# The end of a fused cross-attention and expert layer: stores by tile, softmax sums ahead of values, rows turned by DMA, an indirect gather before the real ones

## What is computed

```python
x = x + tanh(g_xattn) * xattn(layernorm(x), ctx, ctx)      # 16 heads of 32; scores, softmax, values
#     out -> mean over 8 experts of (out @ We[e].T + be[e]) -> @ Wo.T + bo
x = x + tanh(g_ffn) * ffn(layernorm(x))
# ffn: probs = softmax(hs @ w_gate); best = argmax(probs)       (8 experts)
#      the first 100 tokens (in order over all batches) that choose an expert get
#      gate * (hs @ w_expert + b_expert); all others get 0
```

## Time and profile before

| | |
|---|---|
| median of 3 runs | 458.92 us (458.69 to 459.90) |
| the profiled execution | 459.45 us |
| its span | 457.7 us |
| TensorE busy | 431.4 us (94%) |
| DVE busy | 343.7 us (75%) |
| ScalarE busy | 223.4 us (49%) |
| POOL busy | 158.6 us (35%) |
| mean granted TensorE clock | 0.981 |

### The profile page before, as it was taken

The page is one execution under the profiler, slowest core; times in us unless marked ns, Lnnn a source line. Parts: engine busy times, 40 slices in busy tenths (PEclk is TensorE's granted clock), DMA queues, the critical chain, the costliest instruction groups (busy, mean ns, idle before and its releaser), DMA issues.

```text
span 457.7 us, 8305 instructions
## 1 busy us (share of the span) xinstructions
PE 431.4 (94%) x2935; PEld 200.7 (44%) x2935; DVE 343.7 (75%) x670; ACT 223.4 (49%) x278; POOL 158.6 (35%) x147
## 2 busy tenths in 40 slices
PE   5899998899999999999999999999999999499997
PEld 4457564342344344434534443443453444144453
DVE  5448335985597899889879888987983997478873
ACT  4343321556663845666375384656727466451110
POOL 1005899106043319307123430820521161430430
PEclk9997999999999999999999999999999999879999
DMA  8997791048018705923840772593283052230223
GB/s 214 319 391 275 273 399 43 16 108 210 1 30 165 216 19 117 217 93 80 171 176 0 162 179 89 115 189 123 45 168 121 1 117 94 54 90 1 62 65 110
DMA packets 56250, 60.85 MB, mean 133 GB/s; under 512 B 32675, under 2 KB 35887, under 8 KB 56211
## 3 DMA queue, kind: packets, MB, share of 16 engines
q1 hardware_dynamic: 51195, 54.10, 43.5%
q0 software_dynamic: 1536, 3.28, 2.6%
q10 hardware_dynamic: 3480, 2.96, 1.9%
HBM read 29.38 MB, written 12.98 MB: 93 GB/s over the span
## 4 chain that ended last, share of the span: by engine, by line
PE 69%; DVE 12%; issue 10%; ACT 5%; DMA 2%; SPq 0%; DVEq 0%; ACTq 0%; POOLq 0%
PE ps L728 50%; PE ps L405 9%; DVE neg_max L1358 4%; ACT probs L1038 4%; DVE attn L1318 3%; PE ps L367 3%; PE ps L501 3%; DVE q_lo L1352 2%; DMA raw<-in_L_xattn_Wk_dram 1%; DVE rden_both L1313 1%; DMA rows<-out_dram,row_ix 1%; PE ps L989 1%; PE ps L475 1%; PE ps L524 1%; PE ps L931 1%
## 5 line engine op out<-in xcount | busy, mean ns | idle before, releaser
L1038 ACT ACTIVATE probs<-ps 120x2048 f32<-120x2048 f32 x32 | 60.1, 1879 | 41.1 <-PE ps L728 41.1
L1660 POOL TENSOR_TENSOR attn_lo<-attn,attn_hi 128x512 f16<-128x512 f32 x28 | 31.5, 1155 | 114.5 <-ACT attn_hi L1038 114.5
L1358 DVE TENSOR_REDUCE neg_max<-ps 128x16 f32<-128x1920 f32 x32 | 68.6, 2143 | 1.9 <-PE ps L728 1.9
L728 PE MATMUL ps<-xnT_hi,wqT_hi 128*128 128x512 f16 x128 | 48.6, 380 | 1.0 <-issue 0.9
L728 PE MATMUL ps<-mixT_hi,attn_hi 128*128 128x512 f16 x128 | 48.6, 380 | 0.9 <-ACT xnT_hi L1038 0.9
L728 PE MATMUL ps<-mixT_lo,attn_hi 128*128 128x512 f16 x128 | 48.5, 379 | 0.0
L728 PE MATMUL ps<-xnT_lo,wqT_hi 128*128 128x512 f16 x128 | 48.5, 379 | 0.0
L1668 POOL TENSOR_TENSOR xb<-xb,mix_bias 128x512 f32<-128x512 f32 x32 | 39.5, 1265 | 22.4 <-DVE cb_col L1301 22.4
L1605 POOL TENSOR_SCALAR veps<-mv 128x4 f32<-128x4 f32 (+1 forms) x17 | 4.3, 256 | 123.4 <-DVE mv L1247 84.7
L1038 ACT ACTIVATE q_hi<-ps,bias_cols 128x512 f16<-128x512 f32 x32 | 21.9, 684 | 40.1 <-PE ps L728 40.1
L1352 DVE SCALAR_TENSOR_TENSOR q_lo<-ps,bias_cols,q_hi 128x512 f16<-128x512 f32 x32 | 23.9, 746 | 20.7 <-ACT q_hi L1038 20.7
(11 more groups left out here) (242 smaller groups left out, 828.0 us busy)
## 6 DMA issues: line engine op xcount, KB each, us to landing
xb<-in_x_dram SPq DMA_DIRECT2D x8, 1024.0 KB, 5.9
out_dram<-xb SPq DMA_DIRECT2D x7, 1024.0 KB, 6.1
q_stack<-q_hi SPq DMA_DIRECT2D x48, 128.0 KB, 2.4
raw<-in_L_xattn_We_dram SPq DMA_DIRECT2D x5, 1024.0 KB, 12.8
q_stack<-q_lo SPq DMA_DIRECT2D x32, 128.0 KB, 2.4
xb<-in_L_xattn_We_dram SPq DMA_DIRECT2D x3, 1024.0 KB, 11.1
k_stack<-k_scratch SPq DMA_DIRECT2D x8, 360.0 KB, 4.4
ctx_raw<-in_ctx_dram SPq DMA_DIRECT2D x8, 240.0 KB, 7.5
```

Of the source, the lines that this page charges most:

```text
L728: return e.matmul(out_, a, b, start=start, stop=stop, **kw)
L1038: return e.activation(out_, in_, func, **kw)
L1358: e.tensor_reduce(neg_max[:, :, :, g], quad[:, :, 0:NT * SK].rearrange("p j (t s) -> p t j s", t=NT), AX.X, ALU.max, negate=True).then_inc ...
L1660: e.tensor_tensor(attn_lo[:, g, :], attn[:, g, :], attn_hi[:, g, :], ALU.subtract).then_inc(s_alo, 1)
```

## The change

- Stores: batch 6 is stored by tile. Tiles 0 and 1 go ahead of the load of batch 7's shift row, tiles 2 and 3 follow in the next turn of SP's loop.
- TensorE, last batch: `weight_sums` of group 3 stands ahead of `value_sums` of group 2.
- ScalarE: `rden_high` stands ahead of `row_norm` 0.
- Rows 4 to 7 and the four tiles of batch 7 are no longer turned by TensorE. They are split as they lie in SBUF (`row_parts`, `x2_parts`: views of `xn_hi`, `xn_lo` and of `q_stack`), and SP turns them with eight DMA transposes, each for two rows or tiles of one half (`turn_pairs`).
- POOL: `row_ix` is set to 0, and after `add_bias` of batch 7 one indirect gather of row 0 of x is issued (into `rows[:, 0, :]`, written anew by the first real gather); `row_index` and the real gathers wait for it.
- DVE: `enter` is split in `enter_rows` and `enter_places`, the former ahead of `read_places`; `expert_low` is done in two halves, the second after `enter_places` of batch 6; the order of the last batch's steps is another.

```diff
+            def store_tiles(b, tiles):
+                for t in tiles:
+                    e.wait_ge(s_x1, 4 * b + t + 1)
+                    load(out_rows[b][:, t, :], xb[:, b % NX, t, :], s_st)
+
+            def turn_pairs(dst, src, ready, s_):
+                for pair in range(2):
+                    for part in range(2):
+                        e.wait_ge(ready[part][0], ready[part][1] + 2 * pair + 2)
+                        e.dma_start(dst[part][:, 8 * pair:8 * (pair + 1), :],
+                                    src[part].rearrange("p x c -> p (x c)")[:, 8 * P * pair:8 * P * (pair + 1)],
+                                    transpose=True).then_inc(s_[pair][part], 16)
...
-                if 1 <= r < B:
+                if r == B - 1:
+                    store_tiles(B - 2, (2, 3))
+                elif r >= 1:
...
+                    if r == B - 2:
+                        store_tiles(r, (0, 1))
                     e.wait_ge(s_sh, r + 2)
                     load(q_stack[3 * DK:STACK, :, :, :].rearrange("o j g s -> o (j g) s"),
                          shift[:, :], s_rsh)
...
+            e.wait_ge(s_sc, 4 * B)
+            turn_pairs(row_turned, row_parts, ((s_thi, 4), (s_tlo, 4)), s_rowt)
+            turn_pairs(x2_turned, x2_parts, ((s_x2h, 0), (s_x2l, 0)), s_x2t)
...
-                (scores, 0, 3), (weight_sums, 0, 2), (table_rows, -1, 0), (value_sums, 0, 2), (values, 0, 3),
+                (scores, 0, 3), (weight_sums, 0, 2), (table_rows, -1, 0), (weight_sums, 0, 3), (value_sums, 0, 2),
+                (value_sums, 0, 3),
...
-                (row_product, 0, 2), (row_turn, 0, 4), (x2_turn, 0, 0), (row_product, 0, 3), (row_turn, 0, 5),
-                (x2_turn, 0, 1), (row_product, 0, 4), (x2_turn, 0, 2), (row_turn, 0, 6), (row_product, 0, 5),
-                (x2_turn, 0, 3), (row_turn, 0, 7), (row_product, 0, 6), (places, 0, 0), (row_product, 0, 7),
+                (row_product, 0, 2), (row_product, 0, 3), (row_product, 0, 4), (row_product, 0, 5), (row_product, 0, 6),
+                (places, 0, 0), (row_product, 0, 7),
...
             def row_high(_, x_):
+                if x_ >= 4:
+                    e.wait_ge(s_xth, 16 * (B - 1))
+                    e.wait_ge(s_txn, x_ + 1)
+                    act(row_parts[0][0:CAP, x_ - 4, :], row_n[:, x_ % 4, :]).then_inc(s_thi, 1)
+                    return
...
-                (row_norm, 0, 0), (rden_high, 0, 0), (row_high, 0, 0), (row_norm, 0, 1), (attn_high, 0, 0),
+                (rden_high, 0, 0), (row_norm, 0, 0), (row_high, 0, 0), (row_norm, 0, 1), (attn_high, 0, 0),
...
-                (row_high, 0, 2), (row_norm, 0, 3), (row_high, 0, 3), (row_norm, 0, 4), (row_norm, 0, 5),
-                (row_norm, 0, 6), (row_norm, 0, 7), (gate_exp, 0, 0),
-                (row_high, 0, 4), (x2_high, 0, 0), (row_high, 0, 5), (x2_high, 0, 1), (x2_high, 0, 2),
-                (row_high, 0, 6), (x2_high, 0, 3), (row_high, 0, 7),
+                (row_high, 0, 2), (row_norm, 0, 3), (row_high, 0, 3), (row_norm, 0, 4), (row_high, 0, 4),
+                (row_norm, 0, 5), (row_high, 0, 5), (row_norm, 0, 6), (row_high, 0, 6), (row_norm, 0, 7), (row_high, 0, 7),
+                (x2_high, 0, 0), (x2_high, 0, 1), (x2_high, 0, 2), (x2_high, 0, 3), (gate_exp, 0, 0),
...
-                (last_attn_low, 0, 0), (last_attn_low, 0, 1), (divide, 0, 2), (divide, 0, 3), (row_bias, 0, 0),
-                (row_out, 0, 0), (last_attn_low, 0, 2), (last_attn_low, 0, 3), (row_lo, 0, 2), (row_bias, 0, 1),
-                (row_out, 0, 1), (row_lo, 0, 3), (row_bias, 0, 2),
+                (last_attn_low, 0, 0), (last_attn_low, 0, 1), (divide, 0, 2), (divide, 0, 3), (last_attn_low, 0, 2),
+                (last_attn_low, 0, 3), (row_lo, 0, 2), (row_bias, 0, 0), (row_out, 0, 0), (row_lo, 0, 3),
+                (row_bias, 0, 1), (row_out, 0, 1), (row_lo, 0, 4), (row_bias, 0, 2),
+                (x1_tile, 0, 0), (stats2, 0, 0), (moment2, 0, 0), (row_lo, 0, 5), (row_bias, 0, 3),
+                (x1_tile, 0, 1), (route_sum, 0, 0), (stats2, 0, 1), (moment2, 0, 1), (row_lo, 0, 6),
...
             run([B - 2], [(rstd2, -1, 0)] + attn_lows + [(add_bias, 1, 0)])
+            e.wait_ge(s_clr, 2)
+            e.indirect_dma_start(
+                out=rows[:, 0, :], out_offset=None, in_=x_flat[:, :],
+                in_offset=bass.IndirectOffsetOnAxis(ap=row_ix[:, 0:1], axis=0),
+                bounds_check=B * S - 1, oob_is_err=False).then_inc(s_warm, 16)
             run([B - 1], [(rstd2, -1, 0)])
```

More of the change, by code:

```diff
@@ L277, in build @@
         s_x2n = sem("s_x2n")
-        s_x2t = sem("s_x2t")
+        s_x2t = [[sem(f"s_x2t{part}{pair}") for part in ("h", "l")] for pair in range(2)]
+        s_rowt = [[sem(f"s_rowt{part}{pair}") for part in ("h", "l")] for pair in range(2)]
         s_route = sem("s_route")
@@ L302, in build @@
         s_clr = sem("s_clr")
+        s_warm = sem("s_warm")
         s_bex = sem("s_bex")
@@ L596, in run @@
                         step(r + ahead, arg)
-        tail_uses = ([("row", i) for i in range(4)] + [("mix", i) for i in range(4)]
-                     + [("row", 4), ("x2", 0), ("row", 5), ("x2", 1), ("x2", 2), ("row", 6), ("x2", 3), ("row", 7)])
+        tail_uses = [("row", i) for i in range(4)] + [("mix", i) for i in range(4)]
         def tail_bank(kind, i):
@@ L613, in tail_bank_free @@
                 e.wait_ge(s_tlo, i + 1)
[L614 removed]
+            else:
                 e.wait_ge(s_x1, 4 * (B - 1) + i + 1)
[L616 to L618 removed]
         def places_bank(b):
@@ L1434, in read_places, with enter_rows @@
                 link(e.tensor_reduce(place[:, :], place_all[:, :, :], AX.X, ALU.add))
-            def enter(b, _):
+            def enter_rows(b, _):
                 e.wait_ge(s_gt, b + 1)
                 e.wait_ge(s_tb, b)
-                for t in range(NT):
-                    e.tensor_scalar(place_hot[:, t, :], place_iota[:, :], place[:, t:t + 1], None, ALU.is_equal)
                 link(e.tensor_scalar(token[:, :], token_iota[:, :], float(b * S), None, ALU.add))
@@ L1444, in enter, with enter_places @@
                 e.tensor_tensor(entry[:, :, 3, :], choice[:, :, :], wide(rstd[:, 2 + b % 2, :]), ALU.mult)
-                e.tensor_tensor(entry[:, :, 1, :], choice[:, :, :], wide(gate[:, :]), ALU.mult).then_inc(s_en, 1)
+                e.tensor_tensor(entry[:, :, 1, :], choice[:, :, :], wide(gate[:, :]), ALU.mult)
+            def enter_places(b, _):
+                e.wait_ge(s_tb, b)
+                for t in range(NT):
+                    ins = e.tensor_scalar(place_hot[:, t, :], place_iota[:, :], place[:, t:t + 1], None, ALU.is_equal)
+                ins.then_inc(s_en, 1)
             def add_table(b, _):
@@ L1476, in _ @@
                 (route_sum, 0, 0), (stats2, 0, 0), (stats2, 0, 1), (x1_tile, 0, 2),
-                (gate_value, -1, 0), (enter, -1, 0), (expert_low, 1, 0), (x1_tile, 0, 3),
+                (gate_value, -1, 0), (enter_rows, -1, 0), (enter_places, -1, 0), (expert_low, 1, 0),
+                (x1_tile, 0, 3),
             ])
@@ L1560, in _ @@
-                (x1_tile, 0, 0), (stats2, 0, 0), (moment2, 0, 0), (row_bias, 0, 3),
-                (x1_tile, 0, 1), (stats2, 0, 1), (moment2, 0, 1), (route_sum, 0, 0),
-                (x1_tile, 0, 2), (stats2, 0, 2), (moment2, 0, 2), (logit_sum, 0, 0),
-                (normalise2, 0, 0), (normalise2, 0, 1), (x1_tile, 0, 3), (stats2, 0, 3), (moment2, 0, 3),
-                (row_bias, 0, 4), (row_out, 0, 2), (normalise2, 0, 2), (normalise2, 0, 3), (logit_gap, 0, 0),
-                (choose, 0, 0), (row_lo, 0, 4), (x2_lo, 0, 0), (row_out, 0, 3), (row_lo, 0, 5), (x2_lo, 0, 1),
@@ L1566, in _ @@
-                (gate_value, 0, 0), (row_bias, 0, 5), (row_out, 0, 4), (x2_lo, 0, 2), (row_lo, 0, 6), (row_bias, 0, 6),
-                (row_out, 0, 5), (x2_lo, 0, 3), (row_lo, 0, 7), (row_bias, 0, 7), (row_out, 0, 6),
-                (read_places, 0, 0), (last_coefs, 0, 0), (last_bias, 0, 0), (row_out, 0, 7), (last_bias, 0, 1),
-                (last_out, 0, 0), (last_bias, 0, 2), (last_out, 0, 1), (last_bias, 0, 3), (last_out, 0, 2),
-                (last_out, 0, 3),
+                (last_attn_low, 0, 0), (last_attn_low, 0, 1), (divide, 0, 2), (divide, 0, 3), (last_attn_low, 0, 2),
@@ new lines, in _ @@
+                (x2_lo, 0, 0), (x2_lo, 0, 1), (row_bias, 0, 4), (row_out, 0, 2), (normalise2, 0, 2), (normalise2, 0, 3),
+                (row_out, 0, 3), (x2_lo, 0, 2), (x2_lo, 0, 3), (row_bias, 0, 5), (logit_gap, 0, 0), (choose, 0, 0),
+                (row_out, 0, 4), (gate_value, 0, 0), (row_bias, 0, 6), (row_out, 0, 5), (row_bias, 0, 7),
+                (row_out, 0, 6), (read_places, 0, 0), (last_coefs, 0, 0), (last_bias, 0, 0), (row_out, 0, 7),
+                (last_bias, 0, 1), (last_out, 0, 0), (last_bias, 0, 2), (last_out, 0, 1), (last_bias, 0, 3),
@@ L1571, in _ @@
+                (last_out, 0, 2), (last_out, 0, 3),
             ])
```

92 lines of the change are left out of this document (50 added, 42 removed).

## The result

The kernel after takes 452.51 us (median of 4, 451.9 to 453.2) where the kernel before, on the same chip, takes 458.94: a ratio of 0.9861, 95% interval 0.9834 to 0.9887. The profiled execution is 453.2 us, span 451.4, mean granted clock 0.989 (before 459.45, 457.7 and 0.981). The forecast of 452.5 holds almost to the tenth. Its terms hold less well: read against the trace, one is too small by more than a microsecond and two are too pessimistic, and the reason given for the largest is not the right one.

The account below looks back on a forecast made before the run. TensorE was taken as the bound, waiting for the first gather, then busy at full clock from mix tile 0. Terms -1.8 - 0.5 - 4.1 = -6.4 us: 459.45 becomes 453.05, median 452.5; range 451 to 454, whole 449.0 to 455.6.

Parts of the forecast that it names:

- Warm gather: On POOL, an idle-time gather of row 0 removes the first real gather's first-indirect-issue cost: 2.3 us, bounds 0 and 2.3.
- rival (b): POOL's 2.5 us stall stays, perhaps an instruction fetch meeting the real gather again; 2.3 us of gain lost, 454.8; chance 0.13.
- Stores in tiles: Batch 6's split store on SP's queue delays the shift row's load: +0.5 us taken, bounds 0 and 1.4.
- Table: Halving expert_low and moving enter_rows on DVE: gain taken as 0, bound 1.15 us, since table_rows waits behind weight_sums 2.
- Sums ahead of values: TensorE's weight_sums 3 and ScalarE's rden_high go earlier, so the 0.52 us wait behind turn 0 goes.
- Up to mix tile 0: Spread 2 starts 1.8 us earlier, stores' +0.5 included; spread 2 to mix 0 gains 0.5; mix 0 at 409.4.
- rival (a): TensorE's clock never falls, since it stands 2.8 us instead of 5.75 before turn 0: 449.7 us; chance 0.25.
- After mix tile 0: Row and x2 turns leave TensorE, 3.1 us, and the 0.97 us wait ahead of turn 5 goes: -4.1 us.
- rival (c): DVE's or ScalarE's order makes new gaps of 1 to 3 us in the late stretch: 453.5 to 455.5; chance 0.11.
- rival (d): A DMA transpose on SP lands late, beside eight scatters; with a 20 us landing, 463 us; chance 0.04.

Follow-up runs that it names:

- e3_pad: Changed kernel with tile 0 and 1 stores behind the shift row's load and eight one-element POOL memsets replacing the early gather; 450.19 us, ratio 0.9805.
- e6_before_pad: Kernel before with only eight one-element memsets added on POOL ahead of rstd2 of batch 6; 456.65 us, ratio 0.9969.
- e9_first_at_next_fetch: Changed kernel with stores behind the shift row's load, no early gather, and 128 one-element POOL memsets before the last two batches; 453.72 us, ratio 0.9900.
- e5_fetch_back: Changed kernel with stores behind the shift row's load, early gather kept, and 124 one-element POOL memsets in earlier idle time; 450.33 us, ratio 0.9850.

## Why the prediction was right, and where it was not

- **Warm gather** (-2.3 us of stall). The size was right: 3.22 became 1.0. The step "the difference, 2.3 us, I take as the cost of the first indirect issue" failed as a cause. A first indirect issue by itself costs 0.13 to 0.15 us (e3_pad, e6_before_pad); the 2.2 need an instruction fetch at the same place (e9_first_at_next_fetch), and whether they need the first transfer too is open. The chance of 0.13 for rival (b) went to "a fetch that stays"; the fetch was in it, but its place moves with every instruction added to POOL, and I had not counted the three that the change adds. The Trainium skill, "Advanced Engine Details and Errata", section "ISA Cache", has cache lines of 16 KB with 256 instructions. POOL's differ here: the packets are 8 KB, and 128 instructions more brought the stall back (e9_first_at_next_fetch), so the measurement decides.
- **Stores in tiles** (+0.5). The term that was mis-sized: the wait measured 1.67 and 1.96. 0.28 of it stay without the stores and belong to the early gather, to which I had given no such cost; the stores' own 1.4 and 1.7 are at and above my bound of 1.4. I had counted the moving of 512 KB and not that SP itself needs 1.07 us to issue two stores, 0.7 and 0.3 of which fall behind the moment when the shift row is ready.
- **Table** (0). TensorE's steps to the sum of the table show no new wait, and row_ix comes 50.7 us behind the first exponential of batch 6 in the kernels that have the edit and no other delay (e3_pad), 50.8 in the kernel before. As predicted.
- **Sums ahead of values.** The wait ahead of the spreads is gone, as predicted; the reciprocal ran 394.12 to 397.48.
- **Up to mix tile 0.** Predicted 18.0 us from row_ix (391.4, with the +0.5, to 409.4), measured 16.3. TensorE stood 2.6 us, where 2.8 were predicted, and the clock fell again, as predicted against rival (a), but after turn 0 and for less long: the product took 3.8, where I had kept 4.8. That is the second mis-sized step: a slow stretch that starts later cost less of what follows (3.8 and 3.7 us in the two traces of this kernel), though part of it is luck, as the spread among like kernels shows. Spread 2 to mix tile 0 took 3.9 us, so row_lo 2 was worth the whole wait of 0.93 and a little more, not half of it.
- **After mix tile 0** (-4.1). Measured -4.5: TensorE is 3.4 us less busy (41.66 to 38.27), where start-to-start distances gave 3.1, and 1.1 us of idle are gone, where I counted the one wait of 0.97. No list ran late: the logits at 418.25 follow their input at once, x1_tile 0 came 4.35 us after mix tile 0, and rival (c) had no gap to show. Nor had rival (d): the slowest transpose landed in 6.3 us.
- **The total.** Against the trace the errors are +1.2 (stores), +0.7 (upstream of batch 0's first exponential, where the change does nothing), -1.7 (up to mix tile 0), -0.4 (behind it) and +0.3 behind the last matmul. They cancel; the median fell on the forecast partly by luck.

## What to carry to other kernels

A stall with no releaser on an engine that runs long straight programs may be an instruction fetch: before paying for a warm-up, add a few idle instructions and see whether it moves. Ahead of a small load that something waits for, count the issue time of everything put before it on its queue as well as its bytes. Transposes whose inputs are ready 9 us or more before they are needed cost nothing here on an idle DMA queue, and what they took from a TensorE without gaps, 3.4 us of busy time and a wait of about 1, came off that stretch in full. And where executions of one kernel spread over more than the effect, find a row upstream that all kernels share and count from there.

## What the runs showed of the hardware

- An 8 KB packet on q14 at an indirect issue on POOL: 2.2 us at the program's first (four kernels), 0.3 us at a later one that also stood one instruction nearer (e5_fetch_back; which of the two matters is open); the first indirect issue without a packet: 0.15 us. 128 instructions more bring the stall back, 8 take it away.
- A 16 KB load lands in 2.1 us alone, in 2.7 and 2.8 beside a gather of 100 rows, in 3.4 and 4.2 beside that gather and behind two stores of 256 KB.
- After idle TensorE's granted clock fell to 0.50 in every kernel without filler, also behind an idle of 2.6 us, and stayed at 1.00 where matmuls that nobody reads filled the waits (longest wait left: 0.5 us).
- Half-size DMA transposes landed in 3.1 to 6.3 us (whole ones 4.5 to 6.4), with 1.2 to 1.9 us of SP's time for each issue.
